# Cross-attention with layer norm: new instruction orders on all five engines, loads issued by first use, part of the last projections begun early

## The reference, cut to what matters

```python
qh = split_heads(q @ Wq.T + bq)            # q = x, residual = x
kh = split_heads(k @ Wk.T + bk)            # k = v = ctx
vh = split_heads(v @ Wv.T + bv)
scores = einsum('bhqd,bhkd->bhqk', qh, kh) / sqrt(32)
scores = where(mask == 0, -1e9, scores)
e = exp(scores - max(scores)) * mask
probs = e / (sum(e) + 1e-9)
out = merge_heads(einsum('bhqk,bhkd->bhqd', probs, vh)) @ Wo.T + bo
x = out + residual
return (x - mean(x)) / sqrt(var(x) + 1e-05) * ln_g + ln_b
```

## Time and profile before

| | before |
|---|---|
| median of 3 runs | 617.98 us (617.49 to 618.96) |
| the profiled execution | 615.88 us |
| its span | 614.1 us |
| PE (TensorE matmul) busy | 564.5 us, 92% |
| DVE (VectorE) busy | 525.6 us, 86% |
| ACT (ScalarE) busy | 504.6 us, 82% |
| POOL (GpSimd) busy | 437.5 us, 71% |
| granted TensorE clock, mean | 0.985 |
| DMA, mean | 106 GB/s |

### The profile page before, as it was taken

How to read it: one execution, slowest core, us unless ns; L and a number is a source line. 1 busy time by engine, 2 the same in 40 slices (tenths; PEclk the granted TensorE clock), 3 DMA queues, 4 the chain that set the end, 5 groups by cost and what they waited for, 6 DMA issues and landing times.

```text
span 614.1 us, 15264 instructions
## 1 busy us (share of the span) xinstructions
PE 564.5 (92%) x5460; PEld 456.9 (74%) x5460; DVE 525.6 (86%) x801; ACT 504.6 (82%) x2288; POOL 437.5 (71%) x399
## 2 busy tenths in 40 slices
PE   2699398999999999999999999999999999999795
PEld 2588376777878788777877788777878788776574
DVE  4577558789998979898998989898998899899877
ACT  4449669899898989998898989998898999889521
POOL 2704443867588795789778886689678967786787
PEclk9989789999999999999999999999999999999899
DMA  8922730120045310640324412340424312202132
GB/s 310 318 88 57 225 88 1 52 99 3 11 140 188 138 53 10 216 147 3 94 93 155 155 64 75 122 148 3 126 76 141 153 51 104 105 2 99 76 138 102
DMA packets 36198, 64.91 MB, mean 106 GB/s; under 512 B 12443, under 2 KB 14491, under 8 KB 34075
## 3 DMA queue, kind: packets, MB, share of 16 engines
q1 hardware_dynamic: 35979, 63.94, 30.6%
q10 hardware_dynamic: 144, 0.00, 0.0%
HBM read 44.15 MB, written 19.46 MB: 104 GB/s over the span
## 4 chain that ended last, share of the span: by engine, by line
PE 84%; DVE 6%; SPq 5%; DMA 3%; issue 2%; POOL 0%; ACT 0%; DVEq 0%
PE qo_bank L420 54%; PE s_bank L420 17%; PE av_bank L508 11%; DVE E L803 2%; DMA Kd<-TP 2%; PE av_bank L420 1%; DMA Vp<-V_scratch 1%; DVE TP L832 1%; SPq L251 1%; SPq L330 1%; SPq L256 1%; DVE qo_bank L849 1%; DVE bn L855 1%; SPq L304 0%; DVE AT_lo L841 0%
## 5 line engine op out<-in xcount | busy, mean ns | idle before, releaser
L625 ACT ACTIVATE E<-E,neg_max 128x77 f32<-128x77 f32 x1024 | 352.2, 352 | 19.7 <-DVE neg_max L811 19.6
L625 ACT ACTIVATION_READ_ACCUMULATOR E<-E,neg_max 128x1 f32 x1024 | 196.8, 192 | 0.0
L1125 POOL TENSOR_TENSOR E<-E,inv_sum 128x1232 f32<-128x1232 f32 x64 | 145.7, 2279 | 66.6 <-DVE inv_sum L818 66.6
L803 DVE TENSOR_TENSOR E<-s_bank,mask_bias 128x616 f32<-128x616 f32 x128 | 101.3, 791 | 40.7 <-PE s_bank L420 38.9
L420 PE MATMUL s_bank<-Kd,QT_hi 128*128 128x308 f32 x512 | 111.7, 305 | 0.0
L832 DVE STREAM_TRANSPOSE TP<-E 128x1280 f32<-128x1280 f32 x64 | 96.1, 1502 | 4.1 <-PE av_bank L508 3.6
L811 DVE TENSOR_REDUCE neg_max<-E 128x8 f32<-128x624 f32 x128 | 98.5, 781 | 0.4
L420 PE MATMUL s_bank<-Kd,QT_lo 128*128 128x308 f32 x256 | 81.3, 317 | 15.5 <-DVE E L803 11.7
L420 PEld LDWEIGHTS s_bank<-Kd,QT_hi 128*128 128x128 f32 x512 | 84.4, 188 | 4.2
L1143 POOL TENSOR_TENSOR Y<-Y,b_row 128x512 f32<-128x512 f32 x62 | 79.2, 1297 | 4.5 <-ACT Y L642 4.2
L1105 POOL TENSOR_TENSOR xT_lo<-xT_raw,xT_hi 128x1024 fp32r<-128x1024 f32 x30 | 71.7, 2410 | 14.0 <-ACT xT_hi L602 14.0
(11 more groups left out here) (60 smaller groups left out, 790.9 us busy)
## 6 DMA issues: line engine op xcount, KB each, us to landing
Y<-in_x SPq DMA_DIRECT2D x16, 1024.0 KB, 6.1
out_y<-Y SPq DMA_DIRECT2D x64, 256.0 KB, 2.0
xT_raw<-in_xT SPq DMA_DIRECT2D x15, 1024.0 KB, 4.9
Vp<-V_scratch SPq DMA_DIRECT2D x32, 96.0 KB, 2.4
K_scratch<-TP SPq DMA_DIRECT2D x1, 1232.0 KB, 6.8
Y<-in_WqT SPq DMA_DIRECT2D x4, 256.0 KB, 8.4
xT_raw<-in_xT SPq DMA_DIRECT2D x2, 512.0 KB, 6.9
TP<-in_WvT SPq DMA_DIRECT2D x4, 256.0 KB, 7.9
```

What stands on the lines that cost most here:

```text
L625: last = cp(e, e, ACT.Exp, bias=neg_max[:, t, h:h + 1], accum_out=rowsum[:, t, h:h + 1])
L803: tt(E[:, t, :, 0:SK].rearrange("p (g j) k -> p g j k", g=2), s_bank[:, :, 0:GK].rearrange("p g (j k) -> p g j k", j=HG), mask_bias[:, row ...
L1125: nc.gpsimd.tensor_tensor(out=e, in0=e, in1=inv.unsqueeze(2).broadcast_to((P, 2 * HH, SK)), op=ALU.mult).then_inc(probs_ready, 1)
```

## The change

Nothing is computed otherwise, and the number of matmuls of each kind is the same but for the four OUT units that are cut in two. What it does:

- All five tables are new. On TensorE: Q(0, 0) to Q(0, 3) and S(0, 0) now stand before K(2) and K(3); from unit 2 on, an OUT or a Q stands between the last S of one unit and the first S of the next everywhere; AV of the even units 2 to 10 comes one S earlier.
- SyncE: x of block 0 comes before Wq, the mask after x of block 1; load_K(0) is issued before Wv, bv, the zeroing, Wo and the vectors (later_loads); load_rows(0), load_V(0) and load_V(1) follow save_V(0) at once, and load_K(1) and save_K stand behind them.
- GpSimd now casts x of block 1 (XT_hi_1) and the second half of Wq (split_hi_q), and VectorE makes the lo part (XT_lo_first(1, ...)).
- OUT(14, k) is cut in two: OUT_first sums over the half of the heads that unit 14 has made, and OUT over that of unit 15. OUT_first(14, 0) stands before AV(15, 0), OUT_first(14, 1) behind AV(15, 1). OUT(14, 2) and OUT(14, 3) use s_bank in place of qo_bank.

```diff
-                for i in range(2 if b == 0 else 1):
-                    cs = slice(2 * i, 2 * i + 2) if b == 0 else slice(0, C)
-                    sp.dma_start(xT_raw[:, b % 2, cs, :], xT[b, :, cs, :]).then_inc(x_loaded[b % 2], 16)
+                sp.dma_start(xT_raw[:, b % 2, :, :], xT[b]).then_inc(x_loaded[b % 2], 16)
...
             load_half("k", WkT, 0)
+            load_xT_first()
             load_half("q", WqT, 0)
-            load_xT(0)
+            load_xT(1)
             sp.dma_start(mask_i, mask).then_inc(mask_loaded, 16)
-            load_xT(1)
...
+            def later_loads():
+                for c in range(C):
+                    load_w("v", WvT, c)
+                load_row(bv_loaded, bv_row[:, :], bv)
+                zero_V()
+                for c in range(C):
+                    load_w("o", WoT, c)
...
+                elif s == -1:
+                    next_xT(1), load_K(0), later_loads()
...
-                    load_K(1), save_K(), save_V(0), next_xT(2)
+                    save_V(0), load_rows(0), load_V(0), load_V(1)
...
+                    load_K(1), save_K()
...
+        def out_bank(o, k):
+            return s_bank[:, k - 2, :] if split_out(o) and k >= 2 else qo("OUT", o, k)[:, :]
...
+            def OUT_first(o, k):
...
+                if k < 2:
+                    qo_free("OUT", o, k)
+                else:
+                    pe.wait_ge(biased, T2 * NB)
+                OUT_part(o, k, (0, 1), True, False)
...
                 elif s == 21:
-                    OUT(14, 0), OUT(14, 1), OUT(14, 2), OUT(14, 3), OUT(15, 0), OUT(15, 1), OUT(15, 2)
-                    OUT(15, 3)
+                    OUT_first(14, 2), OUT_first(14, 3), OUT(14, 2), OUT(14, 3), OUT(15, 0), OUT(15, 1)
+                    OUT(15, 2), OUT(15, 3)
...
+            def XT_hi_1(i):
+                pool.wait_ge(x_loaded[1], 16)
+                cs = slice(2 * i, 2 * i + 2)
+                nc.gpsimd.tensor_copy(xT_hi[:, 1, cs, :], xT_raw[:, 1, cs, :]).then_inc(x1_hi, 1)
```

More of the change, by code:

```diff
@@ L170, in xattn_program @@
         x_loaded = [sem(f"x_loaded{i}") for i in range(2)]
+        x_first = [sem(f"x_first{i}") for i in range(2)]
+        x1_hi = sem("x1_hi")
+        wq_hi_1 = sem("wq_hi_1")
         rows_in = [sem(f"rows_in{i}") for i in range(2)]
@@ L513, in AV, with OUT_part @@
                     last.then_inc(av_ps, 1)
+            def OUT_part(o, k, cs, first, last):
+                pair, j = o // 2, 4 * (o % 2) + k
+                i, cols = j // 2, slice(j % 2 * P, j % 2 * P + P)
+                pe.wait_ge(at_lo, 4 * (2 * pair + cs[-1] // 2) + i + 1)
+                products = [(a[:, AT_PLACE[2 * pair + c // 2, i], c % 2, cols], w[:, c, :])
+                            for a, w in ((AT_hi, WoT_lo), (AT_lo, WoT_hi), (AT_hi, WoT_hi)) for c in cs]
+                for n, (a, b) in enumerate(products):
+                    done = mm(out_bank(o, k), a, b, start=first and n == 0, stop=last and n == len(products) - 1)
+                return done
+            def OUT_first(o, k):
+                if not has(o):
+                    return
+                if k < 2:
[3 more added lines that the diff above has]
+                OUT_part(o, k, (0, 1), True, False)
             def OUT(o, k):
@@ L665, in _ @@
+                    exponent(1, 1), exponent(1, 2), exponent(1, 3), Q_hi(2, 0), AT_hi_(0, 0), AT_hi_(0, 1)
+                    AT_hi_(0, 2), AT_hi_(0, 3), Q_hi(2, 1)
                 elif s == 4:
-                    XT_hi(3, 1), exponent(1, 2), Q_hi(2, 0), exponent(1, 3), Q_hi(2, 1), exponent(1, 4)
-                    exponent(1, 5), exponent(1, 6), Q_hi(2, 2), Q_hi(2, 3), exponent(1, 7), exponent(2, 0)
-                    exponent(2, 1), exponent(2, 2)
+                    exponent(1, 4), exponent(1, 5), exponent(1, 6), exponent(1, 7), Q_hi(2, 2), Q_hi(2, 3)
@@ L669, in _ @@
+                    exponent(2, 0), exponent(2, 1), Q_hi(3, 0), exponent(2, 2), AT_hi_(1, 0), AT_hi_(1, 1)
+                    AT_hi_(1, 2), AT_hi_(1, 3), exponent(2, 3), Q_hi(3, 1), exponent(2, 4), exponent(2, 5)
+                    Q_hi(3, 2), exponent(2, 6), exponent(2, 7), Q_hi(3, 3), exponent(3, 0)
                 elif s == 5:
-                    Q_hi(3, 0), AT_hi_(1, 0), AT_hi_(1, 1), exponent(2, 3), Q_hi(3, 1), exponent(2, 4)
-                    exponent(2, 5), Q_hi(3, 2), AT_hi_(1, 2), AT_hi_(1, 3), XT_hi(4, 0), XT_hi(4, 1)
@@ L709, in _ @@
                 elif s == 16:
-                    AT_hi_(12, 0), Q_hi(14, 1), LN_scale(10, 2), LN_scale(10, 3), AT_hi_(12, 1)
-                    AT_hi_(12, 2), exponent(13, 4), Q_hi(14, 2), exponent(13, 5), exponent(13, 6)
-                    Q_hi(14, 3), exponent(13, 7), AT_hi_(12, 3)
+                    Q_hi(15, 0), LN_scale(11, 0), LN_scale(11, 1), exponent(14, 2), LN_scale(11, 2)
+                    LN_scale(11, 3), AT_hi_(13, 0), AT_hi_(13, 1), AT_hi_(13, 2), AT_hi_(13, 3), Q_hi(15, 1)
@@ L904, in _ @@
-                    bias(0, 1), row_max(0, 0), row_max(0, 1), split_lo("o", 0), split_lo("o", 1)
-                    split_lo("o", 2), split_lo("o", 3), bias(0, 2), Q_lo(0, 2), Q_lo(0, 3), row_max(0, 2)
-                    bias(0, 3), V_add(0), row_max(0, 3), bias(0, 4), split_lo("q", 2), split_lo("q", 3)
-                    row_max(0, 4), inverse(0, 0), V_add(1), V_add(2), bias(0, 5), row_max(0, 5), turn(0, 0)
-                    bias(0, 6), row_max(0, 6), inverse(0, 1), inverse(0, 2), Q_lo(1, 0), bias(0, 7)
@@ L1236, in _ @@
[L1236 to L1244 removed]
+                    inv_std(s - 4, 0), inv_std(s - 4, 1), add_eps(s - 2, 3), add_beta(s - 4, 0)
```

812 lines of the change are left out of this document (406 added, 406 removed).

## The result

| | before | after |
|---|---|---|
| median of 4 runs beside each other | 617.74 us | 604.06 us (601.94 to 604.55) |
| profiled execution, its span | 615.88, 614.1 us | 604.55, 602.8 us |
| busy PE, DVE, ACT, POOL | 92, 86, 82, 71% | 94, 88, 83, 72% |
| granted TensorE clock, mean | 0.985 | 0.979 |

A forecast was written before the change was run, and what follows sets the result against it. TensorE was taken as the bound in the middle, with the rest its waits at start, middle and end. -11 - 5.5 - 1.5 = -18 from the profiled 615.88 gave 597.9; the median's 2.1 more made 600.0 us, range 592 to 611.

The forecast's parts named there:

- the second rival: Start gives little: four splits pay 6.2 us, later loads land late; A -4, B -4, C -0.5, 609.5 us; chance 0.20.
- term A: Start, up to AV(2, 0): the new order of loads and work saves 11 us; bounds 12.5 and 4.
- the walk: Start: instruction lengths summed along the new order, giving AV(0, 0) at 69.5, AV(1, 0) at 98.5, AV(2, 0) at 128.7.
- To AV(1, 0) ScalarE is the bound: Start, AV(0, 0) to AV(1, 0): ScalarE's instructions set the pace, AV(1, 0) at 98.5 against 110.31, 10.8 us ahead.
- the four splits beside the moved casts: Start: VectorE's splits of Wk's second half beside GpSimd's casts cost at most 6.2 us, mostly covered; costed at 0.
- Term B: Middle, AV(2, 0) to the end of AV(14, 1): OUT between two S removes waits, -5.5 us; bounds -7.2 and +2.
- the 1.7 us held back for new waits: Middle: 7.2 us of waits could go; 1.7 left for new waits because the tables bunch work on ScalarE.
- Term C: End, after AV(14, 1): cut OUT units cover waits, up to 5 us less what goes back, -1.5; bounds -4 and +1.5.
- the mark: The end of AV(14, 1), at 558.64 us in the kernel before, from which the end was measured.
- 4.4 us later AV(15, 0) may start: End: AV(15, 0) may start 4.4 us after unit 15's exponents; AV(15, 1) ends 22.9 us after the mark, before 24.9.
- 1 to 2 us go back: End: TensorE idles about 5 us before AV(15, 0), so AV runs slower and 1 to 2 us are lost.

The follow-up runs named there:

- e5: Changed kernel with only VectorE's end reordered: residual to center of (13, 0) before row_max(15, 6), inverse(15, 3) and turn(15, 2) before residual(13, 2): 602.64 us.
- e6: e5 with center(13, 2) behind turn(15, 3), first halves of OUT(14, 2), (14, 3) before AV(15, 0), and stats to center (15, 2) before residual(15, 3): 602.87 us.
- e7: Changed kernel with the four OUT(14, k) computed whole behind AV(15, 1), each first half directly ahead of its second: 605.18 us.
- e1: Changed kernel with VectorE's three Wo splits moved from beside GpSimd's xT splits to where GpSimd is idle: 602.13 us.
- e11: As e1, but the three Wo splits stand behind inverse(0, 1), beside GpSimd's divisions: 606.24 us.
- e10: Changed kernel with the four casts given to GpSimd (xT of unit 1, second half of Wq) put back on ScalarE: 603.88 us.
- e12: Changed kernel with e1, e2, e6, only Wv loaded ahead of load_K(0), all Wv splits before bias(0, 0), S(0, 2) and S(0, 3) before V(0) and V(1): 596.08 us.
- e4: Changed kernel with S(u, 0) right behind S(u - 1, 7) again in six odd stages, OUT behind both: 612.58 us.
- e8: Changed kernel with e1, e2, e3 and e6 together: 598.09 us.
- e9: Changed kernel with load_K(0) back behind the loads of Wv, Wo and the rows on SyncE: 604.44 us.
- e2: Changed kernel with load_K(1) and save_K ahead of the values' saves and loads on SyncE: 601.62 us.
- e3: Changed kernel with bias and scores of unit 0 ahead of or between Wv's work, and GpSimd's pads ahead of the Wv casts: 601.56 us.

## Why the prediction was right, and where not

The direction and the two places where most was to be gained were right. 600.0 was predicted and 604.06 came. That lies in the wide range, 592 to 611, but just above my own forecast of 595 to 604, at the lower edge of what the second rival gave. The shortfall is that of term A.

- **Term A, the start: -11 predicted, -5.0 measured.** Of that some is scatter. The change's trace has the latest start: with the same tables as far as AV(2, 0), e5, e6 and e7 give -6.4 to -7.3, the mean of the four being -6.4. The keys' and the values' waits went as said, load_K(0) was issued at 20.66 (said 20.7).
  - Up to AV(0, 0) the sum was nearly right, the mechanism only in part. bias(0, 0) began at 33.48, not 31.5, since Wv landed that much later, and S(0, 1) stood 3.44 us for it, which the walk didn't have; the first exponent came at 37.98, not 36.5. turn(0, 0) came at 59.90, not 58.6, AV(0, 0) at 71.25, not 69.5. But VectorE was to stand 4 us for save_K at turn(0, 0), and it stood 0.61: TensorE ran without a wait from 34.32 to 54.4, and bias(0, 7) was over only at 59.3, not at 54.6. That both came to about 59 is luck.
  - The step that failed is "To AV(1, 0) ScalarE is the bound": it summed ScalarE's instructions to 98.5 and left VectorE out. VectorE's Wo splits took 6.87 us in front of bias(1, 4), and ScalarE stood 4.07 us for a maximum. From the start of exponent(0, 7) to AV(1, 0) the walk had 37.7 us and the change took 43.3. e1 took the collision away and took 39.8; the 2.1 us that are left over the walk are in no term. e11 made the collision again elsewhere.
  - I had the price of such a collision in the earlier trace rows and applied it to the four splits beside the moved casts only, where the cost of 0 was right (e10), not to the splits of Wo. (Other than the text on the kernel before first says, GpSimd did take part in splitting x of block 1 there: the earlier trace rows show it making the lo part, beside VectorE's splits of Wk.) e12 has AV(1, 0) at 97.6: the 98.5 can be had, with Wv and the keys both in time.
- **Term B, the middle: -5.5 predicted, -6.5 measured.** Two units take 67.37 us (said 67.5), with no wait of TensorE from 101 us to the last stretch except 0.69 at 514.61, for which the profile names no releaser. So 0.7 of the 1.7 us held back for new waits was needed. e4 shows the mechanism with its price.
- **Term C, the end: -1.5 predicted, +0.2 measured.** The other traces with this end give +0.2 to -0.9. The exponents ended 14.6 us after the mark (summed: 14.4). The step that failed is "4.4 us later AV(15, 0) may start": it was 7.9, as inverse(15, 3) stood behind residual(13, 2), and that behind an OUT(13, 2) which had waited 3.33 us for center(13, 0) and then ran slow. So AV(15) ended 1.6 us later behind the mark than before, where 2.0 earlier was predicted. From there to the last matmul it is 21.8 us for 24.1 (21 was said), and the tail behind it is 7.3 for 6.4, since stats(15, 2) and center(15, 2) come last, as foreseen (6.3 in e8 and e12, where they come earlier). My "1 to 2 us go back" to the clock was right in kind, but the price fell on OUT(13, 2), 5.50 us for 2.80.
- **The second rival** ("the start gives little", 604 to 613) was the nearest in size for A (-4). Part of its reason came true, the later loads landed later than walked; but the four splits cost 0.8 us of the 6.2 it gave them, save_K cost 0.6, and its B of -4 was too small.

What no run tests: the largest wait that went, 8.7 us of AV(0, 0) for the values read back, is gone by the traces alone; no run puts save_V and load_V back where they were.

What stays open: why identical starts differ by up to 2.3 us at AV(1, 0). Half of it is when Wv lands: the last Wv split of VectorE starts between 31.7 and 32.9, and S(0, 1) behind it between 33.2 and 34.3. The other half comes later: from S(0, 1) to AV(1, 0) it takes 70.2 to 71.4 us. There a group behind a wait runs slow in some traces and not in others (Q(2, 1) in the change, e4 and e5, but not in e6 and e7), and why is not shown.

## What to carry to other kernels

When an order is rearranged, walk every engine through the stretch, not only the one that seems to bound it, and price VectorE instructions with two SBUF inputs by what GpSimd does beside them at their new place. A queue that blocks on a semaphore delays everything behind it: put what is needed first after the wait in front of it, but only as many bytes as will have landed when the wait ends. Starting one group earlier at the end pays only as far as the next engine, here GpSimd, has room.

## What was not expected of the hardware

- The collision of VectorE and GpSimd is uneven: 2.29 us for 0.65 on VectorE, and 10.31 for 9.43 in four on GpSimd (5.37 for 4.50 in two beside the divisions).
- Idle time of TensorE mostly cost more than its length. A wait of 0.98 us cost 1.6 (e4). Behind the 3.33 us of idle time OUT(13, 2) ran 5.50 us for 2.80 at a granted clock of 0.50, the lower of the two levels (1.2 of 2.4 GHz), and Q(2, 1) behind the waits before it 4.33 us at 0.61, partly at either. In e7 AV(15) took 5.42 us for 4.02 after 2.33 us of idle time. The windows of the two groups in the changed kernel:

```profile
558.79:564.29 5.50, 5.50 (x13) 4.34 (x14) 3.52 (x4) 4.17 (x20) 2.66 (x3) 0.50 0.03 12
82.87:87.20 4.33, 4.33 (x14) 3.40 (x14) 3.47 (x8) 4.33 (x20) 1.84 (x2) 0.61 0.75 227
```

- The same wait is not always followed by the same clock. Behind the same 3.33 us OUT(13, 2) ran 5.5 us in the change, e1, e7 and e9, and 4.4 to 4.6 in e2, e3, e4, e10 and e11; that is the 1 us by which the ends in the table scatter. And behind the same 2.61 us OUT(15, 2) ran at the full clock in e6, but not in e8 and e12. The windows of e6, e8 and e12:

```profile
587.43:590.50 3.07, 3.06 (x13) 2.52 (x14) 2.19 (x4) 2.31 (x4) 2.84 (x8) 1.00 0.00 0
583.69:588.02 4.33, 4.33 (x13) 3.49 (x14) 2.18 (x4) 2.89 (x4) 4.10 (x9) 0.67 0.00 0
580.66:585.28 4.62, 4.62 (x13) 3.69 (x14) 2.19 (x4) 2.89 (x4) 4.38 (x9) 0.63 0.00 0
```
